# Cross attention and a two-expert FFN on one core: another score layout, a count by ScalarE's sign sums, another order of each body, and both layer normalisations on ScalarE

## What is computed

```python
x = x + xattn(layernorm(x), ctx, ctx, mask)     # Q = .. @ WQ + bQ; K, V from ctx; 16 heads
#   scores = Q K^T * mask (512 queries x 64 keys a head); softmax / sqrt(16); @ V; @ Wp + bp
x = x + ffn(layernorm(x))
#   h = layernorm again, probs = softmax(h*gamma+beta @ Wr + br) over 8 experts
#   expert 0: W1, W2 as given; experts 1..7: one and the same perturbed copy of W1, b1, W2, b2
#   out = probs[0]*(gelu(x@W1+b1)@W2+b2) + (1-probs[0])*(gelu(x@pW1+pb1)@pW2+pb2)
```

## Time and profile before

| | us |
|---|---|
| median of 3 runs | 831.45 (830.91 to 840.44) |
| the profiled execution, its own time | 830.88 |
| span of the profile of that execution | 829.1 |
| PE busy | 716.3 (86%) |
| DVE busy | 530.6 (64%) |
| ACT busy | 295.6 (36%) |
| POOL busy | 282.9 (34%) |

### The profile page before, as it was taken

How to read it: one execution, slowest core, us unless ns; L and a number is a source line. 1 busy time by engine, 2 the same in 40 slices (tenths; PEclk the granted TensorE clock), 3 DMA queues, 4 the chain that set the end, 5 groups by cost and what they waited for, 6 DMA issues and landing times.

```text
span 829.1 us, 16341 instructions
## 1 busy us (share of the span) xinstructions
PE 716.3 (86%) x5986; PEld 642.1 (77%) x5986; DVE 530.6 (64%) x1210; ACT 295.6 (36%) x396; POOL 282.9 (34%) x288
## 2 busy tenths in 40 slices
PE   3525686999989949998998999999893999999996
PEld 2424585798989849898897899888782888888886
DVE  3826666866866885884885794893399444444442
ACT  1301121242542434343443253344441344444442
POOL 2501423344733822834644554534480000000000
PEclk9755566579978978996996998999996999999999
DMA  4851141142161035135134015113020122222211
GB/s 172 163 127 38 51 87 40 44 104 67 46 147 53 25 102 115 31 103 113 32 100 109 10 77 131 36 66 109 34 77 19 58 78 76 76 76 76 76 38 38
DMA packets 128850, 62.61 MB, mean 76 GB/s; under 512 B 101664, under 2 KB 119072, under 8 KB 128800
## 3 DMA queue, kind: packets, MB, share of 16 engines
q1 hardware_dynamic: 128800, 61.94, 27.9%
HBM read 34.51 MB, written 23.09 MB: 69 GB/s over the span
## 4 chain that ended last, share of the span: by engine, by line
PE 68%; DVE 14%; SPq 6%; issue 4%; DMA 4%; POOL 2%; ACT 1%; DVEq 0%; ACTq 0%; POOLq 0%
PE ps_l L343 7%; PE ps_y L343 7%; PE ps_y L344 6%; PE ps_y L345 6%; PE ps_l L345 6%; PE ps_l L344 6%; PE ps_m L615 6%; PE ps_m L691 4%; PE ps_s L343 4%; PE ps_s L603 4%; PE ps_s L345 3%; PE ps_s L344 3%; DVE ind L1255 2%; DMA xa<-in_x 2%; PE ps_m L653 2%
## 5 line engine op out<-in xcount | busy, mean ns | idle before, releaser
L907 ACT ACTIVATE region_b<-ps_l,bias 128x512 f32<-128x512 f32 x128 | 88.0, 688 | 206.9 <-PE ps_l L345 203.8
L343 PE MATMUL ps_y<-w_hi,region_c_hi 128*128 128x256 f32 x512 | 148.1, 289 | 0.0
L344 PE MATMUL ps_y<-w_lo,region_c_hi 128*128 128x256 f32 x512 | 145.7, 284 | 0.0
L345 PE MATMUL ps_y<-w_hi,region_c_lo 128*128 128x256 f32 x512 | 145.6, 284 | 0.0
L1050 POOL TENSOR_TENSOR region_c_lo<-region_b,region_c_hi 128x512 fp32r<-128x512 f32 x64 | 95.3, 1500 | 109.5 <-ACT region_c_hi L910 104.9
L343 PE MATMUL ps_l<-x2s_hi,w_hi 128*128 128x512 f32 x256 | 111.9, 437 | 15.2 <-DVE x2s_lo L1112 14.8
L1255 DVE TENSOR_SCALAR ind<-key,cand 128x2048 bf16<-128x2048 uint16 x124 | 110.9, 937 | 0.1
L345 PE MATMUL ps_l<-x2s_hi,w_lo 128*128 128x512 f32 x256 | 105.7, 413 | 0.0
L344 PE MATMUL ps_l<-x2s_lo,w_hi 128*128 128x512 f32 x256 | 105.7, 413 | 0.0
L1561 DVE TENSOR_TENSOR region_c_lo<-region_b,region_c_hi 128x512 fp32r<-128x512 f32 x64 | 44.3, 692 | 95.8 <-ACT region_c_hi L910 95.8
L343 PEld LDWEIGHTS ps_y<-w_hi,region_c_hi 128*128 128x128 f32 x512 | 98.5, 192 | 3.0
(11 more groups left out here) (171 smaller groups left out, 1230.0 us busy)
## 6 DMA issues: line engine op xcount, KB each, us to landing
acc_scr<-acc SPq DMA_DIRECT2D x8, 514.0 KB, 5.0
acc<-acc_scr SPq DMA_DIRECT2D x8, 514.0 KB, 3.4
xa<-in_x SPq DMA_DIRECT2D x8, 512.0 KB, 5.6
q_scr<-qn_hi SPq DMA_DIRECT2D x16, 256.0 KB, 4.5
q_scr<-qn_lo SPq DMA_DIRECT2D x16, 256.0 KB, 4.9
qs_hi<-q_scr SPq DMA_DIRECT2D x8, 512.0 KB, 4.1
qs_lo<-q_scr SPq DMA_DIRECT2D x8, 512.0 KB, 5.1
x<-in_x SPq DMA_DIRECT2D x32, 128.0 KB, 3.4
```

The costliest lines, as they stand in the source:

```text
L343: eng.matmul(out_ap, a[0], b[0], start=first, stop=False)
L344: eng.matmul(out_ap, a[0], b[1], start=False, stop=False)
L345: return eng.matmul(out_ap, a[1], b[0], start=False, stop=last)
L907: act.activation(g[:, f % 4, :], ps_l[:, f % 2, :], ACT.Gelu_apprx_tanh, bias=bias[:, e, f:f + 1]).then_inc(s["gelu"].handle, 1)
```

## The change

Scores: the high parts of 64 rows of Q stand in partitions 0 to 63 and the low parts in partitions 64 to 127 of one tile `qs`; `kbd` holds the keys' high and low parts in both halves. A score block is then four matmuls of 256 columns. Keys of every batch, the first too, go through `kh_scr`; their eight DMAs carry 32 KB each.

Search: the fourth of the four large counts leaves DVE and PE. ACT computes Sign(cand - key) over the 2048 columns with a running sum, and DVE turns the sum into a count. Candidates are now a half below an integer. `counts` gets one more small instruction.

Layer normalisations: `normalise` moves from POOL to ACT (Identity with a scale and a bias for each partition). POOL's `tick` goes.

Order: all four bodies are rewritten. The last count, total and `decide` of a body move into the next one, `counts(2)` leaves the preamble, the counts are spread out between hidden blocks, `o(0)` and `o(1)` come before `project`, and ACT's fourth exp comes after two gelus.

```diff
-    qs = [sb(f"qs_{n}", [P, DC, S], F32R) for n in ("hi", "lo")]
-    kbd = sb("kbd", [P, 2, DC, HH, CT], F32R)
+    qs = sb("qs", [P, QG, S], F32R)
+    kbd = sb("kbd", [P, 2, QG, H // QG, CT], F32R)
...
             for n in range(2):
+                sp.dma_start(qs[n * HP:(n + 1) * HP].bitcast(F32),
+                             q_scr[n, b].rearrange("h d c r -> (h d) (c r)").rearrange("(m p) s -> p m s", p=HP)).then_inc(q_in.handle, 16)
...
+            for n in range(2):
+                for h in range(H // QG):
+                    to = n * HP + DK * h
+                    sp.dma_start(kbd[to:to + DK, :, :, h, :].rearrange("p n m k -> p (n m) k").bitcast(F32),
+                                 kh_scr[b, DK * h:DK * h + DK].rearrange("p (n k) -> p n k", k=CT)).then_inc(k_in.handle, 16)
...
-        load_first_keys()
...
+        sp.wait_ge(kh_out, 16 * 2 * QG)
+        load_context(0)
...
-            three(pe, ps_s[:, m, :], [t[:, m, j * P:(j + 1) * P] for t in qs],
-                  [kbd[:, n, m].rearrange("p h k -> p (h k)") for n in range(2)]).then_inc(s_product.handle, 1)
+            for g in (2 * m, 2 * m + 1):
+                for n in range(2):
+                    mm = pe.matmul(ps_s[:, m, (g % 2) * D:(g % 2) * D + D], qs[:, g, j * P:(j + 1) * P],
+                                   kbd[:, n, g].rearrange("p h k -> p (h k)"), start=n == 0, stop=n == 1)
...
             turn_probs(i, 0, last)
             h(0)
             if not last:
                 turn_queries_input(i + 1)
+            count(p, 0)
+            count(p, 1)
             h(1)
+            count(p, 2)
+            turn_probs(i, 1, last)
             values(i, 0)
-            c(0, 0, 1, 2, 3)
-            turn_probs(i, 1, last)
-            h(2)
-            t(0)
+            total(p)
             if not last:
                 queries(i + 1)
+            c(0, 0)
             values(i, 1)
             turn_probs(i, 2, last)
-            c(1, 0, 1, 2, 3)
+            c(0, 1)
+            h(2)
+            c(0, 2)
             turn_probs(i, 3, last)
             values(i, 2)
-            t(1)
             h(3)
+            t(0)
+            values(i, 3)
+            h(4)
+            turn_output(i)
             o(0)
-            values(i, 3)
             o(1)
-            turn_output(i)
-            h(4)
+            project(i, 0)
+            project(i, 1)
...
+        def normalise(n, b, src, *tiles):
+            s = ln[n]
+            if 0 in tiles:
+                wait(act, s["shift"], b)
+                wait(act, xT_turned if n == 0 else x2_turned, b - 1)
+            for t in tiles:
+                act.activation(xh[n][:, t, :], src[:, t, :], ACT.Identity, bias=shiftby[n][:, t:t + 1],
+                               scale=rstd[n][:, t:t + 1]).then_inc(s["xhat"].handle, 1)
...
+        def sum_signs(k, rnd):
+
+            wait(act, cand_step, k - 1)
+            act.activation(ind[3][:], key[:, key_of[rnd][3], :], ACT.Sign, bias=cand[:, 3:4], scale=-1.0,
+                           accum_out=signs[:]).then_inc(signs_summed.handle, 1)
...
             turned(i, 0)
             probs(i, 2)
-            probs(i, 3)
+            if not last:
+                high_queries_input(i + 1)
             if not first:
                 router_exp(i - 1)
...
             more_gelu(0)
             turned(i, 1)
+            more_gelu(1)
             if not last:
                 high_queries(i + 1)
+            probs(i, 3)
             turned(i, 2)
-            more_gelu(1)
+            cmp(0)
             turned(i, 3)
             more_gelu(2)
             more_gelu(3)
             high_output(i)
+            if more:
+                normalise(0, i + 2, xa, 0, 1)
             more_gelu(4)
+            if more:
+                normalise(0, i + 2, xa, 2, 3)
...
+            cmp(1)
             more_gelu(5)
+            normalise(1, i, x2, 0, 1, 2, 3)
             more_gelu(6)
...
             copy_x2(i)
+            cmp(2)
+            more_gelu(7)
             high_x2(i)
...
-            if turn:
-                decide(k)
-                second_round()
-            else:
-                decide(k - 1)
-            cmp(0, 0, 1, 2, 3)
             if not last:
                 low_queries_input(i + 1)
+            top_scores(i, 3)
+            counts(p)
+            decide(p)
+            if turn:
+                second_round()
+            cmp(0, 0)
             normalise_output(i, 0)
```

More of the change, by code:

```diff
@@ L626, in turn_output, with project @@
             mm.then_inc(o_turned.handle, 1)
-        def project(b):
-            wait(pe, oT_hi, b)
-            wait(pe, oT_lo, b)
-            for t in range(NT):
+        def project(b, n):
+            if n == 0:
+                wait(pe, oT_hi, b)
+                wait(pe, oT_lo, b)
+            for t in (2 * n, 2 * n + 1):
                 for c in range(DC):
@@ L739, in _ @@
         scores(0, 1, 1)
-        for s in range(4):
+        for s in range(3):
             count(1, s)
@@ L751, in _ @@
         mm.then_inc(route_sum, 1)
-        for s in range(4):
-            count(2, s)
         pe.wait_ge(route_ready, 1)
```

214 lines of the change are left out of this document (97 added, 117 removed).

## The result

The changed kernel takes 784.24 us (median of four runs, 779.89 to 787.88), the kernel before 831.18 us in the same comparison (827.0 to 840.44). The ratio is 0.945, 95% interval 0.938 to 0.952. The forecast was 787. The profiled execution is the fastest of the four, 779.89 us with a span of 778.1; its trace is compared with the span of 829.1 before, of an execution near the median. So the traces lie 51.0 us apart, and the medians 46.9.

The account below looks back on a forecast made before the run. PE bounds the kernel, busy for 86% of the span. Bodies 1, 2, 4, 5 -33.0 us, body 6 -4.3, turn 0, start -6.5, last body -0.5: span 829.1 to 784.8, forecast 787 us, range 769 to 820.

Parts of the forecast that it names:

- The inner body: Bodies 1, 2, 4, 5 and 6: PE's bill of 53.5 us plus 3.5 us idle time and low clock, 57.0 us.
- Counts and scores: PE work removed in each body: 1.6 us by one count fewer a step, 1.5 us by the new score matmuls.
- The walk: One inner body followed through the new programs: the 2.57 us wait for qn_lo goes; h(0) and turn_probs(1) are closest.
- ACT, +14 us a body: ScalarE's added work a body: sign sums 7.6 us, normalisations 4.0, table loads 2.6; none of it on PE's path.
- rival B: Sign sums need their own table loads, 10 us a body, putting ACT's queue on the path: 802 us, chance 0.10.
- Normalisation on ACT: Eight a body, 4.0 us, hidden; before body 1, four take 2.0 us where POOL took 2.77 and a tick.
- The turn: Body 3: the stall of 11 us stays, moved to values(1), so 70 us and no gain.
- Start: Preamble and body 0: body 1 starts 6.5 us earlier, bounds 2 and 9.
- Last body: Body 7: two counts more than before, but a shorter wait for the turn of x2, -0.5 us.
- A: Only the removed work counts; each body keeps its 9.5 us of idle time and low clock: 817 us, chance 0.17.
- C: The clock stays low through the whole first half; a body takes 73 us, the kernel 867 us, chance 0.09.
- D: A wait missed when following the inner body takes 10 us a body or more: no change, 831 us, chance 0.06.

Follow-up runs that it names:

- e1: The changed kernel with the old score layout and its loads put back (three matmuls of 512 columns a block): 797.19 us.
- e2: The changed kernel with the fourth count back on PE and its compare on DVE, without sign sums: 808.14 us.
- e4: The changed kernel with only the new order left (old score layout, four counts on PE, GpSimd normalising): 824.71 us.
- e8: The changed kernel with each of its 31 sign sums made twice on ScalarE: 804.06 us.
- e3: The changed kernel with both normalisations on GpSimd again: 784.54 us.
- e9: The changed kernel with DVE's second_round cut in four parts in the turn and base for expert 0 moved to the turn's end: 774.44 us.
- e7: The changed kernel with PE's hidden block h(2) moved from before to behind values(2): 814.39 us.
- e6: The kernel before with 16 needless matmuls of 512 columns a body added in bodies 1 to 6: 822.34 us.
- e11: e9 with needless matmuls of 512 columns where PE waits, before body 0 (54) and in it (44): 770.08 us.
- e5: The kernel before, in its old order, with the new score layout, sign sums and ScalarE normalisations: 819.44 us (801.3 to 824.8).

## Why the prediction held, point by point

**Direction and size.** 787 against 784.24, inside the range and inside the likeliest case's own. The span of the trace came out 6.7 us lower than the sum, 4 of it because the fastest execution was traced. The error of the sum is made up of terms of both signs: bodies 2, 4, 5 and 6 together 8.7 us too high, start and turn 2.3 and 2.1 too high, body 1 2.5 too low and what follows the start of body 7 4.0 too low.

**The inner body, 57.0 us.** 54.9 to 55.2 in bodies 2, 4 and 5. The bill of 53.5 was good: PE is busy for 24.50 + 29.58 = 54.1 us. The idle time of 1 us was right (30.60 - 29.58). The mis-sized term is the 2.5 us of low clock: it measured 0 in these bodies. Body 1 still has low clock (0.92) and takes 59.5. The 66.1 us from which the bill was worked out stands in no row; the starts give 65.8, and so a bill of 53.2. The starts at 158.72 and 489.82 are read from the chain; PE's timeline has the first transposes 0.15 us earlier, which changes nothing.

**Counts and scores, -3.1 us a body.** As PE's bill this is right (1488 counts, 256 score matmuls, four in 0.55 to 0.56 where 0.51 was taken). As the value of the parts it is wrong. The prediction gave order 9.5 - 3.5 = 6.0 us a body and work 3.1, as terms that add. They don't: the order, worth some 30 us over five inner bodies by its term, brings 9 us alone, and the work, worth 25 by its bill, brings 40 on top of it. The order ends the idle time and the low clock of the first half, but in its second half counts stand between router parts, and with the old counts or the old scores the clock falls there in most bodies (e1, e2, e4). The prediction looked for the longest light run in the first half only and took the second half's clock of 1.00 as given. It held because all of these parts were in the change, and that is luck: nothing in its working says that the second half would keep its clock.

**The walk** (the inner body that the prediction followed). PE's wait for qn_lo is gone. Of the close places neither h(0) nor turn_probs(1) waited in an inner body. DVE and SP were hidden as said: keys cause one wait, in the preamble.

**ACT, +14 us a body.** Sign sums measured 1996 ns and 191 ns for reading the sum, 2.19 against 1.9; a normalised tile 591 ns against 0.5, the table loads as said. Together 8.8 + 4.7 + 2.6 = 16 us, and hidden. e8 shows how narrowly: the place that rival B named, the first `turned` of a body, has 0.35 us of slack and is the one that gives way. The walk had found it free without a number. The trace itself excludes B's cause: table loads stand at exps and gelus alone. The Trainium skill ("ScalarE: Activation LUTs", "Table sets") doesn't name sign among the functions in every set; here it behaves as one. Of the drain of 1.38 us that the same page of the Trainium skill, under "What ACT_TABLE_LOAD costs", adds to a switch, the trace shows nothing: the loads take 1283 ns with 0.3 us of idle time before all fifteen at L924.

**Normalisation on ACT.** Costed at nothing in the bodies, and worth nothing (e3). For the start it was counted with 0.8 us; in e3 body 1 starts 2.4 us later, at 152.3, 1.7 of it before body 0; why more than 0.8 was not looked into.

**The turn, 70 us.** 67.9: the stall of 11 us moved to values(1) as said (11.77 us, from 11.7 to 23.5 us after the turn's start, forecast 11.5 to 22.4). e9 shows that it was the turn's whole surplus over an inner body but for 3 us. The term put the turn at no gain, and it gained 2.1.

**Start, -6.5 us.** -8.8, within the bounds of 2 and 9. The first mask came at 67.46, forecast 67 to 70.

**Last body, -0.5 us.** The wrong sign: it takes 49.7 us to its `mix` against 47.3 before. Its window has a clock of 0.93 against 0.96, and PE waits 1.74 us for a count's indicators: with queries and scores gone, its six counts stand among few dense blocks. That the clock fell for that reason is argued and was not tried. The other 1 us came behind it.

**The rivals.** A (the order keeps the loss) fell with the first half of e4. C (low clock through the first half) fell with a clock of 1.00. D had no wait to show. But C's mechanism is real: e7 is the changed kernel with one block elsewhere, and is 30 us slower. C was priced for the whole first half at the low level, at 867 us; in e1, e2, e4 and e7 the low clock came for 3.4 to 13.7 us a body in bodies 2, 4, 5 and 6, or not at all, and so cost 0 to 7 us.

## What to carry to other kernels

When PE is busy all the time, a bill at the upper level is only half of the question; the other half is where its light matmuls (one column, eight columns, transposes) follow each other, in every stretch of the loop and not only in the one that is slow now. Put dense blocks between them, and try a few needless dense matmuls where PE waits in front of light work: that is a cheap test of what the clock costs, and here it was a gain (e6, e11). Parts of a change that bear on the same run of light work don't add; each has to be tried with the others in place and without them. And where the clock decides, one trace of one body is not enough: look at several bodies of the same program, and at the spread of the runs (e5: 801.3 to 824.8 us).

## What the runs showed of the hardware

The granted clock fell with PE busy for 35.09 of 35.50 us (e4, body 4), so busy time doesn't keep it up by itself; what PE did before it fell were counts of one column and router matmuls of eight. The same program kept 1.00 in e4's body 2. The kernel got faster by 1.3% with 96 matmuls of 512 columns added (e6), and body 0 by 6.1 us with 44 (e11). Two counts of 0.41 us more in a second half made it 4.1 us longer (e2). A sum on the side of an activation adds an instruction of its own, ACTIVATION_READ_ACCUMULATOR, of 191 ns. DVE's base for an expert's output (L1254) takes 879 ns a tile where it took 569 before, with the same shapes; PE doesn't wait for it. Its durations in the changed kernel (ns, min, median, max):

```profile
L1254 DVE SCALAR_TENSOR_TENSOR region_b<-b2row,p,region_b x32: 472/952/1522, 177.1 to 565.1; 128x256 f32<-128x256 f32 x32
```

The traces tell the cause as far as coincidence can: in both kernels each tile of over 650 ns runs beside one of GpSimd's TENSOR_TENSORs for at least 0.67 us (3 of 32 tiles before, 19 after), and the tiles that none overlaps take 472 to 478 ns. No run moved them apart on purpose.
